# A third PSUM bank for the FP4 up product, and the FP4 rounding constants on ScalarE

## The reference

```python
def rmsnorm(x, w): return x * rsqrt(mean(x * x, -1) + eps) * w
# s: linear attention in chunks of 128 tokens (8 heads of 128), then a SwiGLU MLP, 1024 wide
h = rmsnorm(xn, attn_norm_w); x = xn + linear_attention(h, Wq, Wk, Wv, Wo, out_norm_w)
h = rmsnorm(x, mlp_norm_w);   s = x + silu(h @ Wgate) * (h @ Wup) @ Wdown
# g: an FP4 feed-forward network, 704 wide
def fp4_quant_dequant(x):     # groups of 16 along the last dimension
    scale = maximum(max(abs(group)) / 6.0, 1e-12)
    return nearest of (0, .5, 1, 1.5, 2, 3, 4, 6) to abs(group / scale), with its sign, times scale
def fp4_linear(x, w): return fp4_quant_dequant(x) @ fp4_quant_dequant(w).T
g = silu(fp4_linear(silu(fp4_linear(xn, w_gate)) * fp4_linear(xn, w_up), w_down))
```

## Time and profile before

| | |
|---|---|
| Median of 3 runs | 1108.88 us (1108.51 to 1108.95) |
| The profiled execution | 1108.71 us, its span 1107.0 us |
| Mean granted TensorE clock | 0.994 |
| Busy in the span | TensorE 1070.9 us (97%), VectorE 929.2 (84%), ScalarE 508.1 (46%), GpSimd 50.4 (5%) |
| Chain that ended last | TensorE 69%, VectorE 23%, issue 3%, DMA 2%, ScalarE 2% |

### The profile page before, as it was taken

One profiled execution on the slowest core, in us unless ns is written; L12 is line 12 of the kernel. 1 busy time (PEld: TensorE's weight loads), 2 busy tenths in 40 slices (PEclk: granted clock), 3 DMA queues, 4 the chain that ended last, 5 costly groups with the idle time before them and its releaser, 6 DMA issues.

```text
span 1107.0 us, 18697 instructions
## 1 busy us (share of the span) xinstructions
PE 1070.9 (97%) x6830; PEld 967.3 (87%) x6830; DVE 929.2 (84%) x1980; ACT 508.1 (46%) x1392; POOL 50.4 (5%) x70
## 2 busy tenths in 40 slices
PE   9999999999999999999998899999999999999997
PEld 6999999999999889999987688888888888888886
DVE  6889888988889888989677888888888888888886
ACT  6654646546556465564544433333333332332322
POOL 0000000000000000000000000101010100101010
PEclk9999999999999999999999999999999999999999
DMA  7455355553554545535448222322424242333122
GB/s 242 144 166 167 114 183 159 168 172 115 179 172 147 161 149 181 168 115 166 150 146 214 76 92 81 100 91 70 127 77 133 62 133 64 114 95 115 43 74 89
DMA packets 147691, 144.40 MB, mean 130 GB/s; under 512 B 11152, under 2 KB 142608, under 8 KB 147600
## 3 DMA queue, kind: packets, MB, share of 16 engines
q1 hardware_dynamic: 147600, 143.21, 41.2%
HBM read 77.94 MB, written 65.23 MB: 129 GB/s over the span
## 4 chain that ended last, share of the span: by engine, by line
PE 69%; DVE 23%; issue 3%; DMA 2%; ACT 2%; SPq 0%; DVEq 0%
PE ps L257 50%; PE ps L667 5%; PE ps L702 4%; PE ps L708 4%; PE ps L688 4%; DVE work L1473 2%; DVE work L1491 2%; DVE r_v L1495 2%; DVE work L1468 2%; DVE work L1502 2%; DVE r_k L1429 1%; DVE work L1454 1%; DVE work L1450 1%; DVE r_v L1507 1%; DMA moved<-work 1%
## 5 line engine op out<-in xcount | busy, mean ns | idle before, releaser
L257 PE MATMUL ps<-r_k,r_gate_up 128*128 128x512 f32 x768 | 189.6, 395 | 2.7 <-DVE work L1491 2.4
L257 PEld LDWEIGHTS ps<-r_k,r_gate_up 128*128 128x128 f32 x768 | 141.0, 189 | 34.9 <-DVE work L1491 7.9
L257 PE MATMUL ps<-r_o,onT 128*128 128x256 f32 x768 | 108.0, 290 | 0.1
L257 PEld LDWEIGHTS ps<-r_q,r_v 128*128 128x128 f32 x768 | 99.4, 192 | 9.7 <-DVE r_v L1495 4.6
L257 PE MATMUL ps<-r_q,r_v 128*128 128x256 f32 x768 | 103.8, 285 | 2.0 <-DVE r_v L1495 2.0
L930 ACT ACTIVATE work<-ps 128x128 f32<-128x128 f32 x256 | 67.4, 279 | 79.9 <-PE ps L708 79.9
L1069 ACT ACTIVATE r_v<-work 128x512 fp32r<-128x512 f32 x64 | 40.5, 632 | 138.4 <-DVE work L1491 138.4
L257 PE MATMUL ps<-hT,r_k 128*128 128x512 f32 x378 | 103.2, 408 | 0.0
L257 PE MATMUL ps<-hT,r_q 128*128 128x512 f32 x384 | 98.2, 391 | 0.0
L257 PE MATMUL ps<-r_v,hT 128*128 128x512 f32 x384 | 97.4, 390 | 0.0
L257 PEld LDWEIGHTS ps<-r_o,onT 128*128 128x128 f32 x768 | 96.7, 192 | 0.3 <-DVE onT L1209 0.3
(11 more groups left out here) (151 smaller groups left out, 2025.3 us busy)
## 6 DMA issues: line engine op xcount, KB each, us to landing
moved<-work SPq DMA_DIRECT2D x63, 512.0 KB, 2.9
r_gate<-moved SPq DMA_DIRECT2D x252, 128.0 KB, 2.5
kept_h<-work SPq DMA_DIRECT2D x31, 384.0 KB, 2.6
work<-kept_h SPq DMA_DIRECT2D x124, 96.0 KB, 2.3
work<-in_L_attn_hidden_states SPq DMA_DIRECT2D x16, 512.0 KB, 5.4
kept<-work SPq DMA_DIRECT2D x9, 514.0 KB, 4.4
kept_h<-work SPq DMA_DIRECT2D x9, 512.0 KB, 3.8
work<-kept SPq DMA_DIRECT2D x8, 514.0 KB, 6.2
```

The costliest lines, as they stand in the source:

```text
L257: done = pe.matmul(out_ap, a, b, start=first and n == 0, stop=last and n == 2, skip_group_check=skip)
```

## The change

There are two parts. First, the up product of half 1 goes to bank 6 (`B_TURN4`) and that of half 0 stays in bank 5; each waits for `product4` of its own half, one chunk earlier. The first FP4 products of the stage are issued in two parts, with the wait for the last turned weights between them. Second, VectorE still masks the exponents, but signals the result (`power4_ready`) without waiting; ScalarE computes relu(GRID * power - GRID) in place into `grid4` (GRID = 1.5 * 2^22) and signals `grid4_ready`. The addition and the subtraction become three-operand instructions that add GRID back. For this the reciprocal scales are negated. ScalarE's new instruction stands between `hmT_hi(n, 2c)` and `silu_gate(n, 2c+1)`. A column `minus_grid` is filled once by GpSimd.

```diff
+        minus_grid = sb("minus_grid", [P, 1], F32)
...
+        power4_ready, grid4_ready = sem("power4_ready"), sem("grid4_ready")
+        GRID = 1.5 * 2.0 ** 22
...
+        UP4_BANKS = (B_UP4, B_TURN4)
...
+                pool.memset(minus_grid[:, :], -GRID).then_inc(s_const, 1)
                 pool.memset(leaving[:, :, 1, :], 0.0).then_inc(leaving_clear, 1)
-                pool.wait_ge(s_const, 3)
+                pool.wait_ge(s_const, 4)
...
                     for e in halves:
-                        m = 2 * c + e
-                        for w, bank, read, done_sem in ((wgate4, B_GATE4, s_gate4_ready, gate4_done),
-                                                        (wup4, B_UP4, h4_ready, up4_done)):
-                            if m == 0 and w is wgate4:
-                                pe.wait_ge(xT_ready, n * TURNS + KD)
-                            if n or m:
-                                pe.wait_ge(read, n * 2 * CH + m)
+                        m = n * 2 * CH + 2 * c + e
+                        for w, bank, done_sem in ((wgate4, B_GATE4, gate4_done), (wup4, UP4_BANKS[e], up4_done)):
+                            if w is wgate4:
+                                if (c, e) == (0, 0):
+                                    pe.wait_ge(xT_ready, n * TURNS + KD)
+                                if m:
+                                    pe.wait_ge(s_gate4_ready, m)
+                            elif m > 1:
+                                pe.wait_ge(h4_ready, m - 1)
...
-                gate_up4(0, 0)
+                gate_up4(0, 0, (0,))
                 pe.wait_ge(w4_ready, 3 * KD)
+                gate_up4(0, 0, (1,))
...
+                def grid4_on_act(m):
+                    act.wait_ge(power4_ready, m + 1)
+                    act.activation(grid4, grid4, ACT.Relu, scale=GRID, bias=minus_grid[:, 0:1]).then_inc(grid4_ready, 1)
...
                             xT_hi_of(n + 1, range(KD))
+                        grid4_on_act(n * CH + c)
                         silu_gate(n, 2 * c + 1)
...
-                    settled2(dve.tensor_scalar(s, m, 1.0 / FP4_MAX, MIN_SCALE, ALU.mult, ALU.max), mine)
+                    settled2(dve.tensor_scalar(s, m, -1.0 / FP4_MAX, -MIN_SCALE, ALU.mult, ALU.min), mine)
...
-                    settled2(dve.tensor_scalar(r, m, 1.0 - 2.0 ** -23, None, ALU.mult), mine)
+                    settled2(dve.tensor_scalar(r, m, -(1.0 - 2.0 ** -23), None, ALU.mult), mine)
...
-                def quantize_constants(data, mine):
-
-                    settled2(dve.tensor_scalar(grid4.bitcast(U32), data.bitcast(U32), EXPONENT, None,
-                                               ALU.bitwise_and), mine)
-                    settled2(dve.tensor_scalar(grid4, grid4, 1.0, 1.5 * 2.0 ** 22, ALU.max, ALU.mult), mine)
-
-                def quantize_add(data):
-                    dve.tensor_tensor(data, data, grid4, ALU.add).then_inc(dve2, 1)
+                def quantize_constants(data):
+
+                    dve.tensor_scalar(grid4.bitcast(U32), data.bitcast(U32), EXPONENT, None,
+                                      ALU.bitwise_and).then_inc(power4_ready, 1)
+
+                def quantize_add(data, m):
+                    dve.wait_ge(grid4_ready, m + 1)
+                    dve.scalar_tensor_tensor(data, grid4, GRID, data, ALU.add, ALU.add).then_inc(dve2, 1)
...
-                    settled2(dve.tensor_tensor(data, data, grid4, ALU.subtract), mine)
+                    settled2(dve.scalar_tensor_tensor(data, grid4, GRID, data, ALU.add, ALU.subtract), mine)
...
-                SCALE_STEPS, ROUND_STEPS = 5, 5
+                SCALE_STEPS, ROUND_STEPS = 5, 3
...
-                    dve.tensor_tensor(h4[:, c % 2, e * HALF4:(e + 1) * HALF4], ps[:, B_UP4, 0:HALF4],
+                    dve.tensor_tensor(h4[:, c % 2, e * HALF4:(e + 1) * HALF4], ps[:, UP4_BANKS[e], 0:HALF4],
                                       s_gate4[:, e, :], ALU.mult).then_inc(h4_ready, 1)
```

More of the change, by code:

```diff
@@ L619, in _ @@
                     pe.matmul(ps[:, B_O, :], leaving[:, 0, 1, :], leaving[:, :, 1, :], start=True, stop=True)
-                pe.wait_ge(s_const, 5)
+                pe.wait_ge(s_const, 6)
                 for c in range(CH):
@@ L982, in wgate_up_hi @@
                        .then_inc(gu_hi, 1)
-                act.wait_ge(s_const, 5)
+                act.wait_ge(s_const, 6)
                 act.activation(warm[:, :], eps[:, :], ACT.Sqrt)
@@ L1365, in _ @@
                 dve.wait_ge(attn_cleared, 1)
-                dve.wait_ge(s_const, 5)
+                dve.wait_ge(s_const, 6)
                 def attention(b, j, first, final, mine):
@@ L1575, in networks @@
                             xT_lo_of(n + 1, range(KD))
-                        quantize_constants(data, mine)
+                        quantize_constants(data)
                         if LAG4 == 1 and n * CH + c >= LAG4:
@@ L1579, in networks @@
                         mlp_product(n, 2 * c + 1)
-                        quantize_add(data)
+                        quantize_add(data, n * CH + c)
                         mlp_lo(n, 2 * c + 1)
```

## The result

The changed kernel takes 1097.60 us (median of 4 runs, 1096.28 to 1100.12); the kernel before, timed beside it, takes 1108.91 us. The ratio is 0.9896 [0.9874, 0.9919]: 11.3 us faster, where the prediction said 13.3. A second comparison, five rounds, gave 1101.76 against 1110.27, 0.9931 [0.9913, 0.995]: 8.5 us. What the change does per block is the same in both profiles, to 0.03 us; the two differ in the first stage, which the change hardly touches.

The account below looks back on a forecast made before the run. A loop through TensorE and VectorE bounds the kernel. Per block -1.22 - 3.04 + 2.49 = -1.77 us, seven blocks -12.4, first block -0.9, together -13.3: 1095.6 us; forecast 1093 to 1101 (0.73), range 1091 to 1103.

Parts of the forecast that it names:

- The loop and its legs: Networks stage: VectorE and TensorE wait for each other; VectorE's 42.33 us, 0.05 and TensorE's 18.01 make the 60.39 us period.
- TensorE's stops: Second-half up product waits for its bank in chunks 0 and 2, 1.22 us each; TensorE's leg loses one, -1.22 a block.
- The 3.04 us of VectorE's waits: VectorE's waits for TensorE ahead of FP4 gate-up products in chunks 2 and 3; nearly all go, -3.04 us a block.
- The link: Mask, Relu on ScalarE, SiLU queued behind it, MLP product: 0.83 us longer in chunks 1 to 3, +2.49 us a block.
- free in chunk 0: Chunk 0's 0.83 us falls in the 1.83 us VectorE idles before chunk 1's first product, and costs nothing.
- I take no surcharge: VectorE's three-operand addition and subtraction cost no more than two-operand ones; upper bound 0.05 us each, at most 0.3 a block.
- The first block: Other work precedes its chunk 1, so it gains between nothing and a full block's; half is taken, -0.9 us.
- function table: Rival: ScalarE exchanges tables between Relu and SiLU, 1283 ns a load; 15 us slower, about 1124; chance 0.05.
- the banks do nothing: Rival: another wait stops the second up product at the same places; up to 18 us slower, about 1126; chance 0.03.
- The dear link: Rival: a Relu of 1.2 us, or hand-overs slower by 0.3; 6.7 us back, about 1102; chance 0.14.
- The cheap link: Rival: SiLU not held up, TensorE's own work bounds the block at 57.67 us; about 1088; chance 0.05.

Follow-up runs that it names:

- banks alone: Kernel before with only the second bank for the up product and the start in two parts; constants stay on VectorE: 1090.59 us, ratio 0.9827.
- The exchange in chunk 0: Changed kernel with the second MLP SiLU issued ahead of the Relu on ScalarE in chunk 0 of each block only: 1102.39 us, ratio 0.9923.
- that in chunk 3: Changed kernel with the second MLP SiLU issued ahead of the Relu on ScalarE in chunk 3 of each block only: 1090.66 us, ratio 0.9822.
- constants alone: Kernel before with everything of the change but the banks, so up stays in one bank: 1136.69 us, ratio 1.0248.
- before with the column: Kernel before with only the new constant column, its memset and the wait counts raised by one: 1108.98 us, ratio 0.9989.
- SiLU first: Changed kernel with the second MLP SiLU issued ahead of the Relu on ScalarE in every chunk, plus a VectorE wait: 1088.51 us, ratio 0.9809.
- GpSimd's last part tiny: Changed kernel with GpSimd's product of a block's last chunk and all its additions on 4 of 256 columns: 1095.66 us, ratio 0.988.
- GpSimd's last part later: Changed kernel; GpSimd waits before a block's last output product until VectorE has quantized chunk 1 of the next block: 1099.86 us, ratio 0.9923.

## Why the prediction was right, and where it was off

**The loop and its legs held.** Both of TensorE's stops went; its leg measures 16.78 us against 16.79 worked out. The banks alone gained 2.53 us a block.

**The 3.04 us of VectorE's waits went.** In chunks 2 and 3 no wait ahead of line 1515 is left.

**The link was on the path, and free in chunk 0.** The exchange in chunk 0 gained 0.02 us, that in chunk 3 1.15. The Relu took 0.88 us as taken, the wait of VectorE is 1.50, the last down product waits 1.55. A small miss: the spacing from mask to MLP product is 2.02, not 1.95. The hand-over from the SiLU to VectorE is 0.10 us and not 0.03: 3 x 0.07 = 0.21 us.

**The term that was mis-sized is "I take no surcharge"**, though not for the reason weighed there. The form itself costs nothing: the addition takes 0.88 us both ways. The subtraction took 0.55 us more in chunk 1, because GpSimd's product now starts ahead of it. The prediction held to the subtraction's form and did not ask what the longer link would bring it beside. GpSimd's product waits for ScalarE's output. Before, that output waited for TensorE, and GpSimd's product began 2.39 us behind VectorE's MLP product (822.46 and 820.07). The link puts VectorE 0.90 us later, TensorE's part is then ready in time, and GpSimd's product begins 1.70 us behind (815.93 and 814.23), while the subtraction still begins 2.01 us behind. It is the link that does this, not the banks: with the banks alone the subtraction begins at 816.32 and GpSimd's product at 816.71, and the subtraction takes 0.88; with the constants alone the order is 830.02 and 829.72, and it takes 1.43.

Nor is lying beside GpSimd's product enough. Where GpSimd's product starts 0.3 us ahead (changed kernel in both profiles, constants alone, SiLU first in chunk 0 or chunk 3 only) the subtraction takes 1.43 in every block; where it starts 0.4 or 0.6 us behind (before, before with the column, banks alone, SiLU first) the subtraction takes 0.88 or 0.89 in every block. That the order of starting decides is read from these profiles; no run moves GpSimd's product by a few tenths alone. A product on 4 columns that starts 0.3 us ahead leaves the subtraction at 0.89 (GpSimd's last part tiny). The row of the scaling, already 1.31 against 0.89 in other chunks, lay in the trace before and would have warned.

With the hand-overs' 0.21 and the subtraction's 0.55 the period would be 58.62 + 0.21 + 0.55 = 59.38; it is 59.31. The last 0.07 us lie in the product pairs of chunks 2 and 3: back to back they take 0.95 and 0.96 us to the next instruction, where the prediction's 3.04 us of waits left each pair 0.99.

**The whole came nearer to the forecast than the blocks did, and that is luck.** A block gained 1.09 us where 1.77 was forecast. The first comparison's 11.3 us, near the 13.3 forecast, hold some 3 us of scatter from the first stage; the change's worth is about 8 us, and the second comparison gave 8.5.

**The first block** was given half a block's gain, 0.9 us. The profiles do not show its gain. From the first FP4 product to the first residual sum it is 66.20 us before, 65.06 with the column alone, and 65.91 and 65.92 in the two profiles of the changed kernel. The seven distances from the first sum to the last hold the 8.0 to 8.2 us by themselves.

**The rivals.** No function table was exchanged: the trace has two table loads before and after, none between Relu and SiLU. The Trainium skill, "ScalarE: Activation LUTs", section "Table sets: the hidden batching unit", has relu in every set; the trace agrees. That the banks do nothing is refuted by the banks alone, 19.7 us faster. The dear link is refuted by the Relu's 0.88 and hand-overs of 0.03 and 0.10; that the second comparison's 1101.76 lies beside its 1102 has another cause, the subtraction. The cheap link did not happen, but its figure was right: with the SiLU ahead of the Relu the block took 57.66 us, against 57.67 worked out.

**The Trainium skill's advice on relu** ("ScalarE: Activation LUTs", section "Rules for kernel authors"), by which the banks alone would be the better kernel at about 57.7 us a block, came out so in this order of ScalarE's queue: 57.87. The row of the other order limits it: with the SiLU first, the Relu on ScalarE gives 57.66 us a block. The two medians, 1090.59 and 1088.51, were taken on the same chip; their intervals against the kernel before overlap, so the second is not shown to be faster.

**Not settled**: why one block of the constants alone kept its clock behind the same idle time, and how the contention between VectorE and GpSimd chooses which of the two waits.

## What to carry to other kernels

Work moved to an idle engine is priced by its place in that engine's queue, not by its length or by the engine's idle share: 0.88 us of Relu, ahead of a SiLU that was wanted, cost 1.65 us a block (59.31 against 57.66 one place further down); chunk 3 alone gave back 1.15. Follow a moved instruction to the next hand-over of each engine: in a loop through two engines a gain or a loss counts only where the engine that it touches is the late one there. And when an edit shifts one engine against the others, list what it will then run beside, GpSimd's work too.

## What the runs showed of the hardware

Some of VectorE's instructions on SBUF take longer while GpSimd multiplies and adds [128, 256] tiles: 0.88 to 1.43 us for the subtraction, 0.89 to 1.31 or 1.37 for the product with the scale, 0.19 to 0.52 for one on 44 columns. Others do not: beside GpSimd's additions the transpose took 0.84 us (at 819.05 in the changed kernel) and the maximum over groups 0.89 (at 828.81 with GpSimd's last part later), as elsewhere. GpSimd pays as well: its four additions took 4.12 us beside the subtraction and scaling, 2.83 us in the later place, and its product 1.09 us where VectorE's subtraction was under way, 0.74 in the later place. The Trainium skill, "GPSIMD Engine Reference", section "Key points", names contention on the SBUF interfaces that the two share, for VectorE's instructions with two SBUF inputs or in a two-port mode. The runs agree that there is one; the subtraction and the product with the scale have two SBUF inputs, the transpose and the maximum one. They do not tell which interface it is.

TensorE's clock fell after stops of 2.45 us, though not after each (2.13 us for matmuls that take 1.22); it did not fall after those of 1.55 us in the profile shown (1.00 from 640 to 1090 us).

A three-operand instruction of VectorE with a plain number as scalar costs the same as the two-operand one, 881 ns on 704 columns for the addition in either form.
